# A second staging tile in a weight transform, and the softmax reciprocal moved behind its broadcast

## The reference

```python
q = (x @ Wq.T + bq)            # 16 heads of 128
k = x @ Wk.T + bk              # ONE head of 128, shared by all 16
v = x @ Wv.T + bv
scores = einsum('bhtd,bsd->bhts', q, k) / sqrt(128)
scores = where(pos[None, :] < pos[:, None], scores, -1e30)   # strictly causal
attn = softmax(scores) * row_valid      # the first row of all has nothing to attend to
x = layernorm(x + (attn @ v) @ Wo.T + bo)
hidden = silu(x @ W1.T) * (x @ W3.T)    # 8192 wide
hidden = fwht(hidden)                   # Walsh-Hadamard transform over 8192
x = layernorm(x + hidden @ W2.T)
```

## Time and profile before

| | |
|---|---|
| median of the timed runs | 3382.45 us |
| the runs | 3333.5 and 3431.41 us |
| the profiled execution, its own time | 3330.43 us |
| its span, slowest core (core 2) | 3328.9 us |
| spans of the eight cores | 3319.8 to 3328.9 us |
| TensorE busy | 2515.5 us (76%) |
| VectorE, ScalarE, GpSimd busy | 553.0, 693.1, 150.3 us |
| mean granted clock of TensorE, core 2 | 0.860 |
| DMA, whole span | 276.7 MB, 83 GB/s |

### The profile page before, as it was taken

One profiled execution on the slowest core, in us unless ns is written; L12 is line 12 of the kernel. 1 busy time (PEld: TensorE's weight loads), 2 busy tenths in 40 slices (PEclk: granted clock), 3 DMA queues, 4 the chain that ended last, 5 costly groups with the idle time before them and its releaser, 6 DMA issues.

```text
span 3328.9 us, 28154 instructions; the slowest of 8 cores (3319.8 to 3328.9 us)
## 1 busy us (share of the span) xinstructions
PE 2515.5 (76%) x9884; PEld 952.9 (29%) x10080; DVE 553.0 (17%) x760; ACT 693.1 (21%) x1259; POOL 150.3 (5%) x280
## 2 busy tenths in 40 slices
PE   3557663556567888887937999999999999795984
PEld 1112220111111222222313444444444444342432
DVE  0000013333333222221120000000000000002002
ACT  1111111223334445451052111111111110001001
POOL 1110000000000000000000000000000000000000
PEclk8667885567768889898958999999999999897997
DMA  6553334222210000002012222222221214454554
GB/s 192 158 157 99 117 112 141 76 63 64 61 54 1 0 1 0 0 0 76 26 76 91 70 68 70 70 70 70 70 70 64 71 57 130 142 152 149 148 146 145
DMA packets 96462, 276.71 MB, mean 83 GB/s; under 512 B 11716, under 2 KB 11844, under 8 KB 91976
## 3 DMA queue, kind: packets, MB, share of 16 engines
q0 software_dynamic: 34512, 139.48, 14.1%
q1 hardware_dynamic: 61816, 135.43, 12.9%
HBM read 224.54 MB, written 50.33 MB: 83 GB/s over the span
## 4 chain that ended last, share of the span: by engine, by line
PE 70%; DMA 9%; DVE 8%; ACT 7%; issue 5%; SPq 1%; ACTq 0%; DVEq 0%; POOL 0%; POOLq 0%
PE pb L177 67%; DMA W2P<-GA 5%; PE pb L179 4%; DVE GA L241 2%; ACT GA L237 2%; DVE RR L439 2%; ACT GA L423 2%; DMA GA<-X1S 2%; DVE pb L420 1%; ACT GA L654 1%; DMA GA<-XBT 1%; DVE LNS L733 1%; ACT GA L567 1%; ACT GA L548 1%; SPq L250 0%
## 5 line engine op out<-in xcount | busy, mean ns | idle before, releaser
L177 PE MATMUL pb<-GA 128*128 128x512 bf16 x8382 | 2108.9, 394 | 258.0 <-ACT GA L423 64.2
L177 PEld LDWEIGHTS pb<-GA 128*128 128x128 bf16 x8576 | 834.0, 99 | 1482.4 <-issue 657.9
L423 ACT ACTIVATE GA<-pb 128x512 bf16<-128x512 f32 x576 | 340.8, 597 | 518.4 <-PE pb L177 360.2
L179 PE MATMUL pb<-GA,CB 64*64 64x512 bf16 x512 | 137.3, 520 | 353.4 <-DVE GA L241 231.7
L177 PE MATMUL pb<-GA,CB 128*1 128x512 bf16 (+1 forms) x702 | 277.6, 410 | 23.7 <-ACT GA L423 14.1
L654 ACT ACTIVATE GA<-pb 128x512 bf16<-128x512 f32 x128 | 69.6, 595 | 840.4 <-PE pb L177 840.4
L634 DVE TENSOR_TENSOR GA<-GA,pb 128x512 bf16<-128x512 f32 x128 | 82.3, 684 | 915.8 <-ACT GA L631 883.5
L241 DVE CAST GA<-pb 128x512 bf16<-128x512 f32 x128 | 88.5, 692 | 532.9 <-PE pb L179 269.3
L179 PEld LDWEIGHTS pb<-GA,CB 64*64 64x64 bf16 x512 | 36.8, 115 | 448.3 <-issue 448.2
L420 DVE TENSOR_TENSOR pb<-pb,GA 128x512 f32<-128x512 f32 x128 | 89.1, 699 | 422.1 <-PE pb L177 420.1
L177 PEld LDWEIGHTS pb<-GA,CB 128*1 128x1 bf16 (+1 forms) x704 | 58.1, 83 | 214.2 <-issue 199.3
(11 more groups left out here) (46 smaller groups left out, 416.8 us busy)
## 6 DMA issues: line engine op xcount, KB each, us to landing
GA<-W2P SPq DMA_DIRECT2D x256, 256.0 KB, 2.7
GA<-W2T POOLq DMA_DIRECT2D x128, 256.0 KB, 4.3
W2P<-GA SPq DMA_DIRECT2D x128, 256.0 KB, 4.9
GA<-W1S POOLq DMA_DIRECT2D x64, 512.0 KB, 3.8
GA<-W3S POOLq DMA_DIRECT2D x64, 512.0 KB, 3.8
GA<-XBT POOLq DMA_DIRECT2D x8, 2048.0 KB, 13.7
GA<-WQS POOLq DMA_DIRECT2D x4, 2048.0 KB, 11.9
GA<-XOWN SPq DMA_DIRECT2D x1, 8192.0 KB, 33.9
```

The costliest lines, as they stand in the source:

```text
L177: return e.matmul(out, lhsT, rhs, start=start, stop=stop, skip_group_check=True)
L179: return e.matmul(out, lhsT, rhs, start=start, stop=stop, skip_group_check=True, tile_position=tp)
L423: texp = em.op("s", lambda e, qp=qp, slot=slot: e.activation(pbuf[slot], qp[:], AF.Exp, scale=SC), waits=_mx(dep, pbuf_rd[slot]))
```

## The change

Two edits. First, the staging tile becomes a pair, used in turn by the parity of j. The second tile takes 4 KB per partition at offset 116736, which otherwise only the second S1 tile of the later layer norm uses, and that waits for all p0 stores. The evictions of step j now wait for the stores of step j - 2.

Second, r2 is gone from the chain on one partition: the row sum itself is split into a high and a low part and broadcast, and the reciprocal is taken behind the broadcast, on 128 partitions, reading bank 5 and writing recB. It takes the place of ScalarE's copy and stands on VectorE, ahead of the multiplication that uses it.

```diff
-        p0_st = vb(O_P0 + 2 * 4096, 2048)
+        p0_st = [vb(O_P0 + 8192 + k * 4096, 2048) for k in range(2)]
...
-        p0_state = {"i": 0, "wi_rd": [None, None], "st_rd": None, "done": []}
+        p0_state = {"i": 0, "wi_rd": [None, None], "st_rd": [None, None],
+                    "done": []}
...
+            stb = p0_st[j % 2]
...
-                    te = em.op("s", lambda e, ps=ps, q4=q4: e.copy(
-                        p0_st[:, q4 * 512:q4 * 512 + 512], ps[:]),
-                        waits=_mx(tm, p0_state["st_rd"]))
+                    te = em.op("s", lambda e, ps=ps, stb=stb, q4=q4: e.copy(
+                        stb[:, q4 * 512:q4 * 512 + 512], ps[:]),
+                        waits=_mx(tm, p0_state["st_rd"][j % 2]))
...
-            p0_state["st_rd"] = _mx(tda, td)
+            p0_state["st_rd"][j % 2] = _mx(tda, td)
...
-                r2 = em.op("v", lambda e: e.reciprocal(RR[0:1, 512:1024], RR[0:1, 0:512]), waits=_mx(r1))
-                r3 = em.op("v", lambda e: e.tensor_copy(RB2[0:1, 0:512], RR[0:1, 512:1024]),
-                           waits=_mx(r2, st3["rb2_rd"][0]))
-                r4 = em.op("v", lambda e: e.tensor_sub(RR[0:1, 0:512], RR[0:1, 512:1024], RB2[0:1, 0:512]),
+                r3 = em.op("v", lambda e: e.tensor_copy(RB2[0:1, 0:512], RR[0:1, 0:512]),
+                           waits=_mx(r1, st3["rb2_rd"][0]))
+                r4 = em.op("v", lambda e: e.tensor_sub(RR[0:1, 512:1024], RR[0:1, 0:512], RB2[0:1, 0:512]),
                            waits=_mx(r3))
-                r5 = em.op("v", lambda e: e.tensor_copy(RB2[0:1, 512:1024], RR[0:1, 0:512]),
+                r5 = em.op("v", lambda e: e.tensor_copy(RB2[0:1, 512:1024], RR[0:1, 512:1024]),
                            waits=_mx(r4, st3["rb2_rd"][1]))
...
-                        rc = em.op("s", lambda e, rsl=rsl: e.copy(
+                        vrec = em.op("v", lambda e, rsl=rsl: e.reciprocal(
                             recB[rsl], pb[5][:]),
                             waits=_mx(b2, recB_rd[rsl]))
-                        st3["rb_rd"] = rc
+                        st3["rb_rd"] = vrec
                         tv = em.op("v", lambda e, avp=avp, rsl=rsl, dst=dst: e.tensor_mul(
                             dst, avp[:], recB[rsl]),
-                            waits=_mx(rs_mm, rc, qlm if fat else None))
+                            waits=_mx(rs_mm, vrec, qlm if fat else None))
```

More of the change, by code:

```diff
@@ L236, in p0_step @@
                 if eng == "s":
-                    te = em.op("s", lambda e, ps=ps, q4=q4: e.copy(
-                        p0_st[:, q4 * 512:q4 * 512 + 512], ps[:]),
-                        waits=_mx(tm, p0_state["st_rd"]))
-                else:
-                    te = em.op("v", lambda e, ps=ps, q4=q4: e.tensor_copy(
-                        p0_st[:, q4 * 512:q4 * 512 + 512], ps[:]),
-                        waits=_mx(tm, p0_state["st_rd"]))
+                    te = em.op("s", lambda e, ps=ps, stb=stb, q4=q4: e.copy(
+                        stb[:, q4 * 512:q4 * 512 + 512], ps[:]),
+                        waits=_mx(tm, p0_state["st_rd"][j % 2]))
+                else:
+                    te = em.op("v", lambda e, ps=ps, stb=stb, q4=q4: e.tensor_copy(
+                        stb[:, q4 * 512:q4 * 512 + 512], ps[:]),
+                        waits=_mx(tm, p0_state["st_rd"][j % 2]))
                 ps_tok[6] = te
@@ L247, in p0_step @@
             dsts = W2P.rearrange("a t i d -> i t a d", i=128)
-            sA = p0_st[0:64, :].rearrange("p (a d) -> p a d", a=2)
-            sB = p0_st[64:128, :].rearrange("p (a d) -> p a d", a=2)
+            sA = stb[0:64, :].rearrange("p (a d) -> p a d", a=2)
+            sB = stb[64:128, :].rearrange("p (a d) -> p a d", a=2)
             tda = em.op("y", lambda e, j=j, sA=sA: e.dma_start(dsts[2 * j], sA),
```

## The result

The changed kernel is faster: the ratio of its time to that of the kernel before is 0.9373, with a 95% interval of 0.9353 to 0.9392. Its profiled execution took 3127.03 us, against 3330.43 before; the median of its eleven runs is 3126.12 us. (The median of ten runs before, 3412.92 us, contains executions in which the cores of a die had a lower clock than the rest; the ratio leaves those out, and so does all that follows, where some kernels are therefore read on four cores or on few runs.) The forecast was 3112 us against 3330.4, a ratio of 0.934.

The account below looks back on a forecast made before the run. Bound by TensorE's waits on W2P stores and the row-sum reciprocal, plus low-clock work in attention. 143.2 + 51.6 + 0.6 - 9.2 + 32.2 = 218.4 us off 3330.4 gives 3112 us; range 3075 to 3160.

Parts of the forecast that it names:

- The two mechanisms: Second staging tile removes waits on stores, 143.2 us; reciprocal behind the broadcast shortens TensorE's wait, 51.6 us from k = 4.
- the term of the clock: From k = 4 on, TensorE's clock no longer falls behind the broadcast wait: 2.15 us per group, 32.2 us.
- The stores: W2-transform evictions stop waiting for the previous step's stores in K/V, Q and attention; 143.2 us gained.
- the idle of the second quarter: TensorE's idle before the second quarter of odd W2-transform steps falls from 5.73 to 0.9 us.
- the transfer of the wait to step 34 at XOWN: First attention group: step 34 instead of 33 waits for stores queued behind the 8 MB load; 14.6 us gained.
- The new reciprocal: The 128x512 VectorE reciprocal reading PSUM behind the broadcast takes 3.34 to 3.4 us, unscaled by partitions.
- Rival 3: The 128x512 reciprocal costs far more than 3.4 us and becomes the wait behind every broadcast, ending slower; chance 0.02.
- The masks: Reciprocal and product delay mask additions in k = 0 and 1, hidden from k = 2 on; 9.2 us lost.
- The waits before the broadcasts: From k = 4 on, everything behind the reciprocal comes 3.44 us earlier in 15 groups; 51.6 us gained.
- Rival 1: The clock still falls at group boundaries from k = 4 on, losing 32 us, so 3144 us; chance 0.17.
- The first 997 us: Paired W2-transform steps keep their clock level; the mean clock of 482 to 997 us stays near 0.64.

Follow-up runs that it names:

- the experiment: Changed kernel with the reciprocal put back ahead of the broadcast, compared by stretches against the changed kernel; measured 3189.2 us.
- The doses: Changed kernel plus one or two 1x512 VectorE operations in the row-sum chain from k = 4 on; the 15 groups took 441.2 and 458.1 us, against 422.8.
- the spread kernel: Changed kernel with the W2-transform steps cut into quarters issued singly among dense matmuls; ratio 0.8559 to the kernel before, median core 2845.6 us.
- the fourth tile: Changed kernel with the broadcast issued one tile later from k = 4 on; the 15 groups took 410.6 us, against 422.8.

## Why the prediction was right, and where it was not

The two mechanisms were right. The step that failed is the term of the clock, 32.2 us "in full" for 15 groups whose clock would no longer fall: it still fell in 2 to 6 of them, and the term measured 24 us. With that miss alone the time of the changed kernel, 3126 us, still lies inside my range; what puts the measured ratio outside of it is the time that the range was set against (last point).

- The stores. The idle of the second quarter, the transfer of the wait to step 34 at XOWN, and the absence of a new wait on W2T are all as written. Gains of 41.7 and 14.1 us stand beside 40.1 and 12.1. At XOWN 14.8 us stand beside 17.1: I held the landing still at 519.9 us less the shift, but in the denser stretch the load lands 37.6 us after its issue, not 33.9, and step 34 waits 10.35 us where some 6.5 + 0.9 were forecast.
- The new reciprocal. Chosen at the lower bound, 3.34 us, and measured at 3.36. Rival 3 is out.
- The masks. 9.6 us in k = 0 and 1 by the experiment, 9.2 forecast, hidden from k = 2 on, but for 0.4 us.
- The waits before the broadcasts. In the first group of k = 4 3.55 us of idle became 0.16: right. Over the 15 groups 50.8 us became 2.5 (core 0), 48.3 gained where 51.6 were forecast, because I took 3.44 us for each and the mean was 3.39, of which 0.17 stayed.
- The clock from k = 4 on: this is the term that was mis-sized. I took the choice between "the clock still falls" (0) and "it no longer falls" (32.2 us) as one of two cases, and read from the masks that the idle left over would not bring it down. What happens is between them: the stretches of 0.50 that were to be gone are there in 2 to 6 of 15 groups. The 15 groups gained 75.6 us where 83.9 were forecast, on the slowest core 499.3 - 425.4 = 73.9. Of the 75.6, 3.0 are there with the staging tile alone, and 48.3 are the waits; that leaves 24.3 us for the clock. Of the 7.9 us that it gave less than forecast, some 5.3 are falls that stayed (four on the median core, 1.3 us each); the rest is the price of a fall of the kernel before, (24.3 + 5.3) / 15 = 2.0 us where I had worked out 2.15. The doses show that more idle in the boundary brings more falls. Rival 1 was thus partly right, at a quarter of its price.
- The slowest core. I summed terms on one core and compared with the slowest. The profiled execution of the changed kernel has its slowest core 13 us above the median core, that of the kernel before 2 us. Core 2 lost 2.7 us of the 13 in the 15 groups (425.5 against 422.8), 6.3 ahead of them (it reached r1 of (4, 0) at 893.7 us, the others at 879.8 to 890.9) and 3.5 behind them. From r1 of (0, 1) to r1 of (4, 0) it had 304 us at the low level, the others 267 to 291; in the kernel before it was the core with the fewest, 327 against 338 to 351. Why a core has more or fewer in one execution was not tried. That the change sets the cores apart is not shown: in nine other executions of the kernel before (runs of 3327 to 3342 us) the cores lie 11 to 28 us apart, in eight others of the changed kernel 14 to 28. The profiled execution of the kernel before, on which the forecast stands, was an unusually even one.
- The first 997 us. The clock of 482 to 997 us was 0.64, that of the answering 427 to 889 us in the changed kernel is 0.64. That the pairs would not change level on the whole was right; the spread kernel, in which they are gone, shows what they cost.
- The reference time. The forecast of 3112 us was set against 3330.4 us, the profiled execution, which lies at the lower of the two runs shown. Taken as a ratio, 0.934, it is 0.3 points from the 0.9373 measured. Applied to the median of 3382.45 us that was shown, the measured ratio gives 3170 us, above my range, which made no room for that median standing so far above the profiled execution.

## What to carry to other kernels

A buffer that is written once and stored before the next use costs the landing time at every back-to-back use; double it and look for the next thing on the same queue (here the 8 MB load ahead of the store). Where VectorE work on one partition stands ahead of TensorE, the same operation on 128 partitions behind the broadcast costs the same 3.36 us and may be free, unless another piece of work that TensorE wants stands behind it in VectorE's queue: move it to where the queue is empty, and check it at the smallest trip count. Above all, sparse matmuls waiting on evictions cost twice, in idle time and in the clock of what comes next; spread among dense matmuls, the same 64 steps cost 266 us less here. And look at more than one execution before a spread between cores is explained.

## What the runs showed of the hardware that I had not expected

The granted clock answered to small doses. In a boundary (for one of k = 4) with 0.7 us of wait for an exp and 0.16 us for the low part, it fell in 2 to 6 of 15 groups; one operation of 0.78 us in the chain (0.5 us more of idle) made it 9 or 10, two (1.0 us more) all 15, and the falls also grew longer (3.4 us each in the changed kernel, 4.6 with two doses, 6.6 before, by the table). At the fourth tile, with no wait before the broadcasts, it did not fall at all. The Trainium skill (TensorE: Matmul & The Clock Gate, section on a second failure mode, PSUM-queue cycling) says that frequent micro-idles between groups of matmuls can make the clock swing; the doses agree with it. The price that the Trainium skill gives for time at the low level, one half (same page, section on HAM oscillation), would make one fall of 3.4 us cost 1.7 us, an estimate; the cores of the changed kernel show 1.3.
